# A graph network over 200,000 edges: source indices held on chip, four input buffers, products as quarter tiles

## What is computed

```python
def _cgconv(x, src, dst, attr, Wf, bf, Ws, bs):        # layers 0 and 1
    z = jnp.concatenate([x[dst], x[src], attr], axis=-1)   # 64 + 64 + 32
    m = jax.nn.sigmoid(z @ Wf + bf) * jax.nn.softplus(z @ Ws + bs)
    return jax.ops.segment_sum(m, dst, num_segments=N) + x
# each followed by a graph norm over all nodes and a leaky relu
# last layer, row = src, col = dst:
sim = dot(Wh[row], Wh[col]) / maximum(norm * norm, EPS)
prop = segment_sum((base * relu(+-sim))[:, None] * Wh[col], row, num_segments=N)
```

## Time and profile before

| | us |
|---|---|
| median of 3 runs | 11,223.87 |
| lowest, highest | 11,223.36, 11,242.86 |
| the profiled execution's own time | 11,247.99 |
| its span, first to last instruction | 11,246.2 |
| busy: PE, DVE, ACT, POOL | 4,731, 4,361, 2,257, 7,721 |

### The profile page before, as it was taken

One profiled execution on the slowest core, in us unless ns is written; L12 is line 12 of the kernel. 1 busy time (PEld: TensorE's weight loads), 2 busy tenths in 40 slices (PEclk: granted clock), 3 DMA queues, 4 the chain that ended last, 5 costly groups with the idle time before them and its releaser, 6 DMA issues. The chain is left out here.

```text
span 11246.2 us, 89080 instructions
## 1 busy us (share of the span) xinstructions
PE 4731.4 (42%) x15982; PEld 2994.7 (27%) x15982; DVE 4361.2 (39%) x7068; ACT 2257.3 (20%) x3460; POOL 7720.8 (69%) x6875
## 2 busy tenths in 40 slices
PE   0167677777327676676632222222222222222221
PEld 0033333333113333333322222222222222222221
DVE  2433333333323333333334444444444444444445
ACT  0033333333213333333311000110001010000000
POOL 5655555655566666666655888888888888888885
PEclk9978777877657877777765555555555555555555
DMA  7233333333313333333321322232222222222223
GB/s 284 78 95 94 92 96 94 94 95 95 107 52 95 92 94 94 91 96 94 93 61 32 38 36 36 36 36 36 36 36 36 36 36 36 36 36 36 36 36 77
DMA packets 869598, 790.22 MB, mean 70 GB/s; under 512 B 483675, under 2 KB 621803, under 8 KB 868299
## 3 DMA queue, kind: packets, MB, share of 16 engines
q0 software_dynamic: 398432, 244.82, 17.2%
q1 hardware_dynamic: 461928, 480.85, 14.0%
q10 hardware_dynamic: 9218, 64.36, 1.4%
HBM read 547.94 MB, written 241.38 MB: 70 GB/s over the span
## 5 line engine op out<-in xcount | busy, mean ns | idle before, releaser
L663 POOL DMA_INDIRECT by_src<-arena,put_idx x1568 | 2495.6, 1592 | 481.0 <-issue 480.7
L589 POOL DMA_INDIRECT G<-h_rows,idx x1568 | 1549.2, 988 | 936.0 <-issue 479.6
L589 POOL DMA_INDIRECT G<-in_x,idx x1470 | 1450.8, 987 | 1004.0 <-issue 530.7
L764 PE MATMUL ps_gv<-ident,arena 128*128 128x128 f32 x1568 | 385.5, 427 | 3731.1 <-issue 3673.5
L589 POOL DMA_INDIRECT G<-wh_rows,idx x1568 | 1534.6, 979 | 484.7 <-issue 421.6
L764 PEld LDWEIGHTS ps_gv<-ident,arena 128*128 128x128 f32 x1568 | 307.6, 224 | 3793.5 <-issue 3773.3
L1040 DVE TENSOR_TENSOR_SCAN xd_t<-same,xd_t,ps_inj 128x512 f32<-128x512 bf16 x588 | 751.6, 1278 | 1307.3 <-remote 896.8
L716 PE MATMUL ps_gv<-attr,w_attr 65*128 65x512 f32 x1568 | 1067.3, 817 | 351.6 <-DMA attr<-in_attr_t 291.8
L719 PE MATMUL ps_gv<-arena,w_src 128*128 128x512 f32 x1568 | 1011.2, 781 | 0.0
L1183 DVE TENSOR_SCALAR put_idx<-arena,drop 128x8 int32<-128x8 f32 x196 | 45.6, 233 | 2289.3 <-DMA by_src<-arena,put_idx 2289.3
L1063 DVE TENSOR_SCALAR arena<-ps_gv 128x512 f32<-128x512 f32 x392 | 267.3, 682 | 1671.7 <-remote 1197.4
(11 more groups left out here) (162 smaller groups left out, 7079.5 us busy)
## 6 DMA issues: line engine op xcount, KB each, us to landing
inj<-first_edge_rows SPq DMA_DIRECT2D x588, 256.0 KB
running_sums<-arena SPq DMA_DIRECT2D x392, 256.0 KB
same<-same_dst SPq DMA_DIRECT2D x1176, 64.0 KB
first_edge_rows<-zeros ACTq DMA_DIRECT2D x56, 896.0 KB
attr<-in_attr_t SPq DMA_DIRECT2D x392, 128.0 KB
same_sum<-same_dst SPq DMA_DIRECT2D x784, 64.0 KB
G<-h_rows,idx POOLq DMA_INDIRECT x1568
G<-wh_rows,idx POOLq DMA_INDIRECT x1568
```

The costliest lines, as they stand in the source:

```text
L589: pool.indirect_dma_start(out_, None, table_in, bass.IndirectOffsetOnAxis(ap=index, axis=0)).then_inc(s, 16)
L663: pool.indirect_dma_start(acc_d[a], bass.IndirectOffsetOnAxis(ap=put_idx[:, buf, k:k + 1], axis=0), put[:, buf, k * D:(k + 1) * D], None, ...
L764: mm = pe.transpose(spread[:, buf, k], src_f[:, buf, k:k + 1].to_broadcast([P, P]), ident[:])
```

## The change

Source indices are loaded once, into `src_idx`, and stay there for all layers; POOL's loops over groups are written out, so that each gather names its columns directly. `inj`, `same`, `attr` and `G` have four buffers (`NB`), loops take four groups per trip, one copy of the flags serves both scans, and SP loads rows two groups ahead and attributes and flags one ahead. The products are written as 64 x 64 quarters: the attributes stand twice in their tile, and in `G` pairs of slots are swapped (`k ^ 1`), so that the source rows of a half stand on the partitions of the other half, and a quarter of the array adds the products of `dst` rows or `src` rows to the output half that they belong to. Gate and value of different halves are written at the same time. The biases become operands of the operations behind. In the last layer the products are as they were.

```diff
+NB = 4
+TRIPS = GROUPS // NB
+        src_idx = sb("src_idx", [P, GROUPS * SLOTS], I32)
-        idx = sb("idx", [P, 2, SLOTS], I32)
-        inj = sb("inj", [P, 2, SLOTS * D])
-        same = sb("same", [P, 2, COLS], BF16)
-        same_sum = sb("same_sum", [P, 2, COLS], BF16)
-        attr = sb("attr", [2 * DA + 1, 2, COLS])
-        G = sb("G", [P, 2, SLOTS * D])
+        inj = sb("inj", [P, NB, SLOTS * D])
+        same = sb("same", [P, NB, COLS], BF16)
+        attr = sb("attr", [P, NB, COLS])
+        G = sb("G", [P, NB, SLOTS * D])
...
+            load(src_idx[:], src_g, s_srcs)
...
                 def load_rows(h, buf):
-                    sp.wait_ge(s_scan, done(layer, h, buf, 2))
+                    sp.wait_ge(s_injt, done(layer, h, buf, NB))
...
+                def load_flags(h, buf):
+                    sp.wait_ge(s_scan if layer == 2 else s_sumt, done(layer, h, buf, NB))
...
-                pipeline(sp, (load_idx, -1), (load_rows, -1), (load_ahead, 0), (load_attr, 1), (load_again, 2),
-                         (store_sums, 4))
+                pipeline(sp, (load_rows, -2), (load_ahead, -2), (load_attr, -1), (load_flags, -1), (store_sums, 4))
...
-                with pool.Fori(0, PAIRS) as i:
-                    for buf in range(2):
-                        gather_group(i, buf)
+                for g in range(GROUPS):
+                    gather_group(g)
...
+                        wait(s_gt if layer < 2 else s_used, done(layer if layer < 2 else 0, h, buf, NB))
+                        at = k ^ 1 if layer < 2 else k
+                        gather(G[:, buf, at * D:(at + 1) * D], table_in, src_of(g, k), s_gath[buf])
...
+                def quarter(buf, k, rows, cols, w, moving, start, stop):
+
+                    top = slice(rows * D, (rows + 1) * D)
+                    return pe.matmul(ps_gv[cols * D:(cols + 1) * D, buf % 2, k], w[top], moving[top], start=start,
+                                     stop=stop)
+
+                def nodes_quarters(buf, k_of_rows, stop):
+                    for rows in range(2):
+                        k = k_of_rows[rows]
+                        for cols in range(2):
+                            w, moving = (w_dst, xd_t) if rows == cols else (w_src, xs_t)
+                            mm = quarter(buf, k, rows, cols, w[:, layer, k], moving[:, buf % 2], False, stop)
+                            if not stop:
+                                mm.then_inc(s_half, 1)
+                    return mm
...
+                    for rows in range(2):
+                        for cols in range(2):
+                            quarter(buf, rows, rows, cols, w_attr[:, layer, rows, cols], attr[:, buf], True, False)
...
+                    nodes_quarters(buf, (0, 1), False)
...
                 def products(h, buf):
...
+                    pe.wait_ge(s_half, h * (4 * NB) + 4 * (layer * GROUPS + buf + 1))
+                    nodes_quarters(buf, (1, 0), True).then_inc(s_gates, 1)
...
-                pipeline(pe, (turn_rows, 0), (products, 1), (turn_sums, 2))
+                pipeline(pe, (turn_rows, 0), (products_attr, 1), (turn_sums, 3), (products, 1))
...
-                pipeline(act, (copy_rows, 0), (gates, 1), (copy_sums, 2), steps=steps, per=6)
+                pipeline(act, (copy_rows, 0), (copy_sums, 3), (gates, 1), steps=steps, per=3 * NB)
```

More of the change, by code:

```diff
@@ L103, in two, with each @@
             return [sem(f"{name}_{i}") for i in range(2)]
+        def each(name):
+            return [sem(f"{name}_{i}") for i in range(NB)]
         def dram(name, shape, dt=F32):
@@ L185, in gnn @@
         tile = carve()
-        dst_now, dst_was, src_i, dst_i = (tile(GROUPS * SLOTS, dt=I32) for _ in range(4))
+        dst_now, dst_was, dst_i = (tile(GROUPS * SLOTS, dt=I32) for _ in range(3))
         deg, deg_tmp = tile(GROUPS * SLOTS), tile(GROUPS * SLOTS)
@@ L423, in pipeline @@
                     steps.begin(i - head, per)
-                step(i, 0)
-                step(i, 1)
+                for buf in range(n):
+                    step(i, buf)
             if steps:
@@ L428, in pipeline @@
                 steps.begin()
-            for k in range(2 * tail, 2 * pairs + max(lags)):
-                step(k // 2, k % 2)
+            for k in range(n * tail, n * trips + max(lags)):
+                step(k // n, k % n)
             if steps:
@@ L517, in load_same @@
-                def load_same(tile_, s, g, buf):
-                    for half in range(2):
-                        load(tile_[half * D:(half + 1) * D, buf],
-                             same_groups[ds(g + half * GROUPS, 1), :].to_broadcast([D, COLS]), s[buf])
-                def load_again(h, buf):
-                    sp.wait_ge(s_sumt, done(layer, h, buf, 2))
-                    load_same(same_sum, s_same_sum, h * 2 + buf, buf)
+                def load_rows(h, buf):
+                    sp.wait_ge(s_injt, done(layer, h, buf, NB))
+                    load(inj[:, buf], inj_groups[ds(h * NB + buf, 1)].rearrange("a p c -> p (a c)"), s_load[buf])
@@ new lines, in load_flags @@
+                def load_flags(h, buf):
+                    sp.wait_ge(s_scan if layer == 2 else s_sumt, done(layer, h, buf, NB))
+                    for half in range(2):
+                        load(same[half * D:(half + 1) * D, buf],
+                             same_groups[ds(h * NB + buf + half * GROUPS, 1), :].to_broadcast([D, COLS]), s_flags[buf])
+                def load_ahead(h, buf):
+                    if buf % 2 and layer < AHEAD:
+                        sp.wait_ge(s_gt, done(layer, h, buf, NB))
+                        load(G[:, buf, (SLOTS - 2) * D:(SLOTS - 1) * D],
+                             ahead_pairs[:, ds(h * (NB // 2) + buf // 2, 1)].rearrange("p a f -> p (a f)"),
+                             s_ahead_in[buf // 2])
@@ L526, in store_sums @@
+                def load_attr(h, buf):
+                    sp.wait_ge(s_gates, done(layer, h, buf, NB))
+                    load(attr[:, buf], attr_t[ds(h * NB + buf, 1)].rearrange("a k c -> k (a c)"), s_attr[buf])
                 def store_sums(h, buf):
-                    g = h * 2 + buf
+                    g = h * NB + buf
                     sp.wait_ge(s_sums, done(layer, h, buf))
-                    load(sums_groups[ds(g, 1)].rearrange("a p c -> p (a c)"), sums[:, buf], s_stored[buf])
@@ L591, in gather_ahead @@
             def gather_ahead(begin, end):
-                with pool.Fori(begin, end) as i:
+                for i in range(begin, end):
                     for buf in range(2):
-                        wait(s_aidx[buf], i * 16 + 16)
                         wait(s_ahead_st[buf], i * 16 + 16)
                         for c in range(CH):
-                            gather(agg[:, buf, c * D:(c + 1) * D], x, get_nodes[:, buf, c:c + 1], s_ahead[buf])
+                            pair = (i * 2 + buf) * CH + c
+                            gather(agg[:, buf, c * D:(c + 1) * D], x, src_of(2 * pair + 1, SLOTS - 1), s_ahead[buf])
+            pool.wait_ge(s_srcs, 16)
             pool.wait_ge(s_end_idx, 1)
@@ L659, in add_run @@
                         half = a // (ACCS // 2)
-                        if a % (ACCS // 2) == 0 and (run or buf or not at_start(h)):
+                        if a % (ACCS // 2) == 0 and (run or g):
                             wait(s_added[half], added(h, buf, run))
@@ L892, in copy_put @@
                 put_before(act, h, buf)
[L893 removed]
+                nc.scalar.copy(put[:, buf % 2], ps_out[:]).then_inc(s_put, 1)
             def src_squares(h, buf):
```

285 lines of the change are left out of this document (135 added, 150 removed).

## The result

| | before | changed | ratio, 95% interval |
|---|---|---|---|
| beside each other (set 1), median of 4 | 11,233.37 | 10,884.19 | 0.9689 [0.9666, 0.9711] |
| forecast (median of 3: 11,223.87) | | 10,180 (10,050 to 10,700) | |
| later, in set 5 (e13), median of 24 and 4 | 10,234.43 | 10,188.44 | 0.9949 [0.9932, 0.9965] |

The change won 349 us, a third of the forecast. The third row is needed to understand the others. In the first set and three of these the kernel before took 11,225 to 11,354 us; in the other three it took 10,220 to 10,239 us, the same program. I call these sets *late* and *on time*, for what their traces show. Times are compared within a set; where two sets are compared, it is by their ratios, and the text says so.

The account below looks back on a forecast made before the run. POOL was taken as the bound, held up in layers 0 and 1 by index loads. Removing 563, 466 and 36 us (setup) and adding 20 for code took 11,248 to 10,203 us, 10,180 for the median; range 10,050 to 10,700.

Parts of the forecast that it names:

- 563 and 466 us are real waits: Layers 0 and 1: POOL's idle time beyond the 0.30 us gaps before gathers was real waiting, 563 and 466 us.
- the waits name a DMA: Layers 0 and 1: POOL waits for the load of a group's 8 indices, 410 us in 73 waits of layer 0.
- the 1,029: Layers 0 and 1: POOL's waits of 563 and 466 us together, all counted as won if POOL never waits.
- The prediction's chain: Layers 0 and 1: POOL's stall idles PE, PE returns at half speed (13 instead of 7.0 us a group), delaying SP's queue.
- Rival D: Group loops: SP or a PSUM buffer holds them at 12.5 us, only setup is won, 11,190 us; chance 0.04.
- A: Whole kernel: POOL bounds it after the change, 10,180 us (10,050 to 10,330); chance 0.71.
- 1, indices: Index loads: one 784 KB load replaces 588 small ones, POOL's index waits go, SP has one issue fewer a group.
- 2 and 3, buffers and order: Group loops: four buffers cover PE being 10 us behind; SP's issues fall from 8.5 to 5.5 a group.
- 4, quarter tiles: PE's products: twelve staggered quarters take 5.7 us a group against 5.3, 7.6 with transposes, hidden under POOL's 9.65.
- C: PE's products: quarters run one after another, 15.6 us a group at today's clock, 12,350 us in all; chance 0.08.
- 5 and 6: Bias moved out of the product costs nothing; POOL's loops written out cost 20 us for loading code, bounds 0 and 130.
- Setup: Before the loops: the first put moves from 227 to 191, when the clearing ends, 36 us gained, bounds 0 and 42.6.

Follow-up runs that it names:

- e13: The changed kernel, run again beside the kernel before in an on-time set: 10,188 us, ratio 0.9949.
- e1: Kernel before with only source indices kept on chip and POOL's loops written out; late set: 10,926 us, ratio 0.9648.
- e12: The kernel before, unchanged, run for a profile in an on-time set: 10,231 us, ratio 0.9996.
- e2: Changed kernel with its products back as six 128x128 products a group instead of quarter tiles; late set: 10,804 us, ratio 0.9541.
- e14: The kernel of e2 (changed kernel with full 128x128 products), run again in an on-time set: 10,212 us, ratio 0.9980.
- e3: Changed kernel, quarter tiles kept, without the source-row gathers of layers 0 and 1; late set, timing only: 8,805 us.
- e4: Changed kernel with six 128x128 products and without the source-row gathers of layers 0 and 1; late set, timing only: 8,961 us.
- e7: Kernel of e2 with POOL writing zeros to a scratch tile in place of each gather in layers 0 and 1; late set: 9,021 us, ratio 0.8039.
- e5: Kernel of e2 with rows, flags and attributes loaded only for the first four groups in layers 0 and 1; late set: 10,723 us, ratio 0.9556.
- e6: Kernel of e2 with only the destination rows' products, two of six, in layers 0 and 1; late set: 10,717 us, ratio 0.9551.
- e16: Kernel of e2 with PE waiting for a semaphore POOL raises after rows land, not the gathers' own; late set: 10,816 us, ratio 0.9530.

## Why the prediction was wrong, step by step

**What bounds.** The step that failed is the first: "563 and 466 us are real waits", and "the waits name a DMA", from which the sum takes 563 + 466 us as won once the index load is gone. The first half held for that trace. The second took the name for the cause. With the load gone 341 and 312 us of waits stay, on PE's late signals. That an engine waits for a load which is issued late says nothing about what made the load late. The trace of before held two signs that I passed over. Right behind the index load of the earlier trace rows SP needs 1.36 us to its next issue. And PE is idle through 2032 to 2036, although its results of 2029.88 and before are first used at 2033:

```profile
2033.19 1.28 DVE L1040 TENSOR_TENSOR_SCAN xd_t<-same,xd_t,ps_inj 128x512 f32<-128x512 bf16 x1 [5.75 <-remote]
2033.21 0.58 ACT L839 COPY arena<-ps_out 128x512 f32<-128x512 f32 x1 [2.86 <-remote]
```

In the late condition the index part is worth 395 us against the 1,029 (e1); on time the whole change is worth 46 us, and 14 us of waits in the loops name an index load at all (e12 against e13).

The prediction's chain, a stall of POOL makes PE idle, PE comes back at half speed, and its lateness holds SP's queue, doesn't hold either. PE is idle from 2029.88 while DVE and ACT wait for what it has finished: `ps_inj` is complete at 2023.98 and first read at 2033.19. And on time PE's clock dips as well (0.85 and 0.82), with 14 us of such waits.

**Rival D** ("the wait only changes its name") had 0.04 and was nearest: the waits did change their name, in two thirds of their size. **A** came true to 8 us in e13 (10,188 us against 10,180), by luck: the kernel before took 10,234 us there, so its gain of 1,045 us did not exist, 46 us did. What was right in it is the floor, POOL back to back with 0.30 us before each gather, which e12 and e13 both come near.

**1, indices:** above. **2 and 3, buffers and order:** with 5 they bring 1.1%, 120 us, in late sets (e1 to e2), presumably by letting POOL run through more of the stalls, which no run takes apart; nothing on time (e12 and e14 differ by 0.2%, and the first gather of layer 0 comes 25 us sooner in e14).

**4, quarter tiles:** I took 5.7 us for twelve quarters, one staggered behind the other. They run four side by side: eight passes from 2016.13 to 2017.04, and in the rows of e13 below from 1509.82 to 1510.91, so 0.9 to 1.1 us for each set of eight and 2.9 us in all, near the lower bound of 2.6.

```profile
1509.82 0.72 PE L712 MATMUL ps_gv<-xd_t,w_dst 64*64 64x512 f32 x1
1509.83 0.72 PE L712 MATMUL ps_gv<-arena,w_src 64*64 64x512 f32 x2
1509.84 1.13 PE L712 MATMUL ps_gv<-xd_t,w_dst 64*64 64x512 f32 x2
1510.38 0.59 PE L712 MATMUL ps_gv<-arena,w_src 64*64 64x512 f32 x2
1510.39 0.59 PE L712 MATMUL ps_gv<-xd_t,w_dst 64*64 64x512 f32 x1
1510.91 0.66 PE L695 MATMUL ps_inj<-ident,inj 128*128 128x128 f32 x4
```

The rows agree with what the Trainium skill says ("TensorE: Matmul & The Clock Gate", Part 3: tiles at different places run together), and the trace decides for it against my staggering. The trace also agrees with the drain that the Trainium skill names ("TensorEngine Tiling (Array Packing)", Key Properties). In the late profile, at full clock, no weights are loaded for 0.81 us before a set of full-size transposes that follows quarters, and they are loaded only as the transposes start. In the kernel before, where full-size products precede them, it is 0.24 us, and the weights come 0.43 us ahead of the transposes at 2022.91. The changed kernel, then the kernel before:

```profile
2012.62 0.56 PEld L748 LDWEIGHTS ps_out<-ident,arena 128*128 128x128 f32 x4 [0.81 <-issue]
```
```profile
2022.48 0.20 PEld L729 LDWEIGHTS ps_out<-ident,arena 128*128 128x128 f32 x1 [0.24 <-issue]
```

Most of the 0.81 us lies beside the quarters' own passes: the four transposes start 0.96 us after the last eight passes did. What I left out is that the split gives PE a wait on itself. The third four add to what other rows of the array are writing, so they wait for the second four's signal. With signals on time that costs nothing that shows, and e13 is 0.2% faster than e14. Where signals are late, it is 731 us of waits from 600 to 2,700 us, and the changed kernel's ratio is 1.5% worse than e2's, over two sets. It also gives PE eight matmul signals a group where there were four, and they came one after the other in the rows above; which of the two costs the time was not tested. PE's clock is lower with quarters in either condition (0.76 against 0.80 late, 0.80 against 0.85 on time, layer 0), where PE has less to do. So the product part of the change is likely what it lost against e2, by a mechanism that was none of the rivals (C blamed the array's pace).

**5 and 6:** POOL written out costs nothing that shows. I charged 20 us; the idle time of its last loop is 477.9 and 480.9 us where the earlier trace rows have 484.7 and 481.0, though 80 packets came over the instruction queue, not 17. The bias costs nothing that shows.

**Setup:** 36 us forecast; 491.3 - 476.4 = 15 us in the late pair, 26 in the other. The first put came at 213.8 and 205.7 us, not at 191: the ahead gathers themselves end at 202 to 205, later than the 191 at which I took the clearing to end, and in the late run the clearing ends later still:

```profile
201.45 0.95 POOL L582 DMA_INDIRECT agg<-in_x,src_idx  x1 [0.30 <-issue]
213.84 1.00 POOL L613 DMA_INDIRECT first_edge_rows<-stage,put_nodes  x1 [11.45 <-DMA first_edge_rows<-zeros]
```

## What to carry to other kernels

The name of a wait is what ended last, and not its cause: before pricing its removal, look whether the engine behind it works at its usual pace, here SP's distance between issues and the time from a matmul's end to the first use of its result. Count the semaphore events against the signals too. If many engines wait for "remote" in a program of one core, or start microseconds after their input's recorded end, the trace holds a disturbance that the change won't remove, and the forecast needs a case for it. A split that adds signals on an engine's own path is cheap only while signals are: nothing on time, likely 80 to 166 us here.

## What the runs showed of the hardware that was not expected

- The same program takes 10,220 to 10,239 us in some sets and 11,225 to 11,354 us in others, each steady within 0.5%. The difference lies nearly all in the two loops with gathers and PE work side by side: 2,448 and 2,478 us against 1,923 and 2,058; the last loop takes 4,989 and 4,976 us.
- In the late sets PE's semaphores rise 2 to 9 us (medians of the kernel before, of the signals that have an event) after the recorded end of the matmul; PE's own longest wait for one is 23.6 us. This comes with POOL's gathers (e3, e4, e7) and needs neither most of the direct loads (e5), nor most of PE's products (e6), nor PE's wait on the gathers (e16). While POOL gathers there, a fifth to a half of all semaphore events are missing from the trace, in the last layer too, and hardly any where it doesn't gather. In the last layer, with as many gathers and as many adds in twice the time, they are on time. What tells this layer from the others, what part of the chip is shared, and whether it is the chip or its state, stays open.
- Four 64x64 fp32 products in different quarters of the array, two passes each, take 0.9 to 1.1 us together, near the 0.88 us of one full-size product (two passes of 0.44 us); without gathers PE's busy share is 1.00 with full products at 6.88 us a group (e4) and 0.77 with quarters at 6.48 us (e3).
